# First stage: normalised input at the head of VectorE's turn, mean square a step later, one silu session a pair; scan: the next pair's first inputs formed ahead

## The reference

```
x = x + attn_a(layernorm(x));  x = x + ffn(layernorm(x))
x = x + attn_b(layernorm(x));  x = x + ffn(layernorm(x))

# attn_a, after the input projection (z, xBC, dt):
xBC = silu(causal_conv4(xBC) + conv_b);  x, B, C = split(xBC)
dt = softplus(dt + dt_bias);  A = -exp(A_log)
Y = ssd(x * dt, A * dt, B, C) + D * x        # 4 heads of 64, state 16, by sums over tiles of 128
y = rmsnorm(Y * silu(z)) * norm_w;  return y @ W_out.T

# attn_b (the scan), 256 channels x 16 states:
dt = softplus(x @ Wdt.T + bdt + dt_bias)
A_bar = (1 + dt*A/2) / (1 - dt*A/2);  B_bar = dt / (1 - dt*A/2)
state_t = A_bar_t * state_{t-1} + B_bar_t * B_t * xi_t;  out_t = sum_s state_t[s] * C_t[s]
y = layernorm(out * silu(z)) * gamma + beta;  return y @ Wout.T
```

## Time and profile before

| | |
|---|---|
| time, three runs | 2639.4, 2646.31, 2657.2 us; median 2646.31 |
| the profiled execution | 2651.16 us, its span 2649.4 us |
| busy, share of the span | PE 83%, VectorE 75%, ScalarE 70%, GpSimd 58% |
| mean granted TensorE clock | 0.928; first stage 0.90, scan 0.84 |
| first stage | 0 to 300 us: a turn takes 31.3 to 33.4 us |
| feed-forward | 300 to 1098 us, and 1856 to 2649 us |
| scan | 1098 to 1856 us: a turn takes about 92 us |

### The profile page before, as it was taken

The page is one execution under the profiler, slowest core; times in us unless marked ns, Lnnn a source line. Parts: engine busy times, 40 slices in busy tenths (PEclk is TensorE's granted clock), DMA queues, the critical chain, the costliest instruction groups (busy, mean ns, idle before and its releaser), DMA issues. The chain is left out here.

```text
span 2649.4 us, 46209 instructions
## 1 busy us (share of the span) xinstructions
PE 2192.8 (83%) x13308; PEld 1124.7 (42%) x13308; DVE 1996.1 (75%) x5421; ACT 1856.4 (70%) x4745; POOL 1543.0 (58%) x1364
## 2 busy tenths in 40 slices
PE   5888789999999999667777767776799899999997
PEld 2555445455555555222222222222355455555553
DVE  4666477777777776388998989898677777787774
ACT  3555277778777777488687777776677777777774
POOL 1233276556665665177787677676565556665652
PEclk8999799999999999788888888889999999999999
DMA  3000000000000000000000000000000000000000
GB/s 129 1 0 1 4 13 13 10 14 12 13 13 14 12 9 14 0 0 1 1 1 1 0 1 0 0 1 0 13 13 13 9 14 12 13 17 17 21 13 17
DMA packets 12209, 30.04 MB, mean 11 GB/s; under 512 B 2240, under 2 KB 2240, under 8 KB 11584
## 3 DMA queue, kind: packets, MB, share of 16 engines
q1 hardware_dynamic: 11968, 27.41, 3.8%
HBM read 8.52 MB, written 2.10 MB: 4 GB/s over the span
## 5 line engine op out<-in xcount | busy, mean ns | idle before, releaser
L517 POOL TENSOR_TENSOR arena<-arena 128x512 f32<-128x512 f32 x256 | 325.0, 1270 | 444.8 <-DVE arena L1530 444.8
L575 POOL TENSOR_TENSOR arena<-arena 128x512 f32<-128x512 f32 x256 | 327.7, 1295 | 127.2 <-ACT arena L1257 118.5
L523 POOL TENSOR_TENSOR arena<-arena,SR 128x512 f32<-128x512 f32 x256 | 285.3, 1114 | 109.5 <-ACT SR L1139 108.6
L1610 DVE TENSOR_TENSOR_SCAN arena<-arena,psum 128x512 f32<-128x512 f32 x256 | 311.0, 1215 | 3.2
L929 PE MATMUL psum<-BS,tabs 96*128 96x512 bf16 x384 | 146.1, 442 | 197.1 <-DVE arena L1610 195.3
L997 PE MATMUL psum<-arena,first 128*128 128x512 f32 x512 | 288.8, 653 | 10.9 <-POOL arena L566 10.6
L1536 DVE TENSOR_REDUCE SM<-arena 128x8 f32<-128x512 f32 x256 | 175.6, 686 | 155.9 <-ACT arena L1129 145.5
L530 POOL TENSOR_TENSOR P<-P,RS 128x512 f32<-128x512 f32 x256 | 270.3, 1056 | 35.5 <-DVE RS L1457 35.1
L1129 ACT ACTIVATE arena<-psum 128x512 f32<-128x512 f32 x256 | 151.4, 591 | 186.6 <-PE psum L853 186.5
L853 PE MATMUL psum<-rest,HA 128*128 128x512 f32 x512 | 267.3, 604 | 0.4 <-DVE HA L1445 0.4
L807 PE MATMUL psum<-HN,rest 128*128 128x512 f32 (+1 forms) x384 | 197.0, 640 | 56.0 <-ACT arena L1122 51.0
(11 more groups left out here) (223 smaller groups left out, 5290.8 us busy)
## 6 DMA issues: line engine op xcount, KB each, us to landing
arena<-arena SPq DMA_DIRECT2D x128, 128.0 KB, 2.3
rest<-in_rest SPq DMA_DIRECT2D x1, 4183.0 KB, 20.9
X<-in_x SPq DMA_DIRECT2D x1, 2048.0 KB, 9.0
out<-X SPq DMA_DIRECT2D x8, 256.0 KB, 2.3
tabs<-in_tabs SPq DMA_DIRECT2D x1, 1216.0 KB, 11.5
first<-in_first SPq DMA_DIRECT2D x1, 875.5 KB, 4.5
```

The source lines that it names most:

```text
L517: nc.gpsimd.tensor_tensor(CQ[:, n % 2, :], CQ[:, n % 2, :], SQN[:, n % 2, :], ALU.add).then_inc(f_rope, 1)
L523: nc.gpsimd.tensor_tensor(heads, heads, SR[:, n % 2, :].unsqueeze(2).to_broadcast([128, HEADS, DH]), ALU.mult).then_inc(f_qk, 1)
L575: nc.gpsimd.tensor_tensor(WU[:, k % DEEP, :], RG[:, k % DEEP, :], U[t.j % 2][:, k % 2, :], ALU.mult).then_inc(m_wu, 1)
L1610: v.tensor_tensor_scan(HS[:, k % DEEP, :], AB[:, k % DEEP, :], B_BANK[k % 2], 0.0, ALU.mult, ALU.add).then_inc(m_hs, 1)
```

## The change

In the first stage:
- VectorE forms x times dt and XN at the head of the turn, ahead of the first mask and the first MM product; before, they stood behind MM and the D term.
- PE's mean square (L687) moves from steps 3 and 4 to steps 4 and 5, so that its second half stands behind the second x projection.
- ACT's silu of x moves from step 7 to step 12, into the session of B, C and z; the table loads at step 7 go.

In the scan:
- POOL forms WU of steps 0 and 1 of the next pair at the end of a turn, each ahead of one of the last two odd products.
- PE spreads the next pair's B for steps 0 and 1 and C for state 0 at the end of a turn, ahead of the last three sums.
- VectorE's CEN, HN and the block of L1651 and L1653 move one step later (2 to 3, 8 to 9, 11 to 12).

```diff
@@ POOL, scan
+            def weighted_input(t, k, pair=0):
+                t.wait_ge(m_rg, STEPS, k + 1, pair=pair)
+                t.wait_ge(m_vb, STEPS, k + 1 - DEEP, pair=pair)
+                if k == 0:
+                    t.wait_ge(m_u, 1, 1, pair=pair)
+                nc.gpsimd.tensor_tensor(WU[:, k % DEEP, :], RG[:, k % DEEP, :], U[(t.j + pair) % 2][:, k % 2, :],
+                                        ALU.mult).then_inc(m_wu, 1)
+
             def pool_turn(t):
                 for k in range(STEPS):
                     if t.states:
-                        t.wait_ge(m_rg, STEPS, k + 1)
-                        t.wait_ge(m_vb, STEPS, k + 1 - DEEP)
-                        if k == 0:
-                            t.wait_ge(m_u, 1, 1)
-                        nc.gpsimd.tensor_tensor(WU[:, k % DEEP, :], RG[:, k % DEEP, :], U[t.j % 2][:, k % 2, :],
-                                                ALU.mult).then_inc(m_wu, 1)
+                        if k >= 2:
+                            weighted_input(t, k)
...
-                if t.states:
-                    odd_times_c(t, NS - 2)
-                    odd_times_c(t, NS - 1)
+                for late in range(2):
+                    if t.after:
+                        weighted_input(t, late, pair=1)
+                    if t.states:
+                        odd_times_c(t, NS - 2 + late)
@@ PE, first stage
             def a_pe_ending(t, h):
-                if h in (3, 4):
-                    half = h - 3
+                if h in (4, 5):
+                    half = h - 4
@@ PE, scan
             def pe_turn(t):
                 if t.states:
-                    spread_b(t, 0)
-                    spread_c(t, 0)
-                    spread_b(t, 1)
                     spread_c(t, 1)
...
-                    if t.states and k >= 2:
+                    if t.states and 2 <= k < STEPS - 1:
                         accumulate(t, k - 2)
+                if t.after:
+                    spread_b(t, 0, pair=1)
+                    spread_c(t, 0, pair=1)
+                    spread_b(t, 1, pair=1)
                 if t.states:
-                    accumulate(t, STEPS - 2)
-                    accumulate(t, STEPS - 1)
+                    for k in range(STEPS - 3, STEPS):
+                        accumulate(t, k)
@@ ACT, first stage
-                elif h == 7:
+                elif h == 12:
                     for k in range(2):
                         t.wait_ge(a_cx, 8, 4 * k + 4, pair=1)
                         A(XA[side][:, k, :], XA[side][:, k, :], ACT.Silu, bias=F("a_convb", k, k + 1)).then_inc(a_act, 1)
-                    nc.scalar.preload_act_table_set(EXP_LN)
-                elif h == 12:
@@ VectorE, first stage
                 for h in range(16):
+                    if t.states and h == 0:
+                        x_times_dt(t)
+                    if t.after and h == 0:
+                        a_dve_beginning(t, h)
                     if t.states and h % 2 == 0:
...
-                    if t.states and h == 0:
-                        x_times_dt(t)
                     if t.before:
                         a_dve_ending(t, h)
-                    if t.after:
+                    if t.after and h:
                         a_dve_beginning(t, h)
@@ VectorE, scan
-                if k == 2:
+                if k == 3:
                     t.wait_ge(ln_mean, 1, LN_M + 1, pair=1)
...
-                elif k == 8:
+                elif k == 9:
                     t.wait_ge(ln_rs, 1, LN_M + 1, pair=1)
...
-                elif k == 11:
+                elif k == 12:
                     t.wait_ge(m_exp, 1, 1, pair=1)
```

More of the change, by code:

```diff
@@ L926, in _, with spread, spread_b, spread_c @@
             pe.wait_ge(f_x, PAIRS)
-            def spread(t, s, column, dst, done):
-                mm(dst, T16("sel", 128 * column, 128 * column + 128, p=96), BS[t.j % 2][:, :],
+            def spread(t, column, dst, done, pair):
+                mm(dst, T16("sel", 128 * column, 128 * column + 128, p=96), BS[(t.j + pair) % 2][:, :],
                    start=True, stop=True).then_inc(done, 1)
-            def spread_b(t, k):
-                t.wait_ge(m_hs, STEPS, k - 1)
+            def spread_b(t, k, pair=0):
+                t.wait_ge(m_hs, STEPS, k - 1, pair=pair)
                 if k == 0:
-                    t.wait_ge(m_bs, 3, 3)
-                spread(t, k, k // 2, B_BANK[k % 2], m_bb)
-            def spread_c(t, s):
-                t.wait_ge(m_pce, NS, s - 1)
-                spread(t, s, NS + s, C_BANK[s % 2], m_bc)
+                    t.wait_ge(m_bs, 3, 3, pair=pair)
+                spread(t, k // 2, B_BANK[k % 2], m_bb, pair)
+            def spread_c(t, s, pair=0):
+                t.wait_ge(m_pce, NS, s - 1, pair=pair)
+                spread(t, NS + s, C_BANK[s % 2], m_bc, pair)
             def half_sum(k, weight, source, done):
```

## The result

The changed kernel took 2620.69 us in the median of four runs, against 2650.53 for the kernel before beside it: a ratio of 0.988 (95% interval 0.985 to 0.990), 29.8 us less. I had forecast 33. In a later group of runs the same kernel came to 0.990 (0.987 to 0.994). The profiled execution took 2621.68 us, 29.5 less than the one of before.

The account below looks back on a forecast made before the run. VectorE was taken as nearly full in the scan, no engine full in the first stage. First stage 16 us less, scan 17.2 less (21.2 less 4.0), together 33: from 2646.3 to 2613 us, range 2595 to 2630.

Parts of the forecast that it names:

- first stage: First-stage turns: 16 us less in all, bounds 6 and 22; net 2.1 us in each of six turns.
- scan's border: Borders between scan turns: VectorE's 2.83 us wait goes at five, 7.0 us more at two jumps back; together 21.2 us less.
- shifted beginning: CEN, HN and L1651 a step later in the scan: waits are one 4.0 us slack that only moves; costs 4.0 us.
- L1669's holds: Scan's maximum stays long in five of seven turns; rival that it falls the other way, 2595 or 2620 us, chance 0.10.
- XN at the head: First stage: x times dt and XN fit into VectorE's early waits, so all behind comes 2.1 us sooner a turn.
- the stall: First stage: PE's 1.65 us wait ahead of L656 goes, and full clock is expected where it was 0.59.
- Mean square later: First stage: moving L687's second half behind x projection L662 removes VectorE's wait there, 1.0 us a turn.
- One session: First stage: silus of x in the later session cost 1.4 us a turn on the path; 0.4 us LM wait goes.
- the jumps' 1.3: Scan's two jumps back: VectorE's own instruction fetch comes to light, 1.3 us exposed at each.
- The four places that I listed: Scan turn's middle: where VectorE would wait instead: 1.5 us at WU(11), 1.6 at L1651, 1.7 at WU(17), 1.1 at WU(19).
- The rival in which the waits vanish: Scan turn's middle: the shift does remove VectorE's waits, some 24 us more gained, 2589 us; chance 0.06.
- The slower rival: Scan: POOL holds HN and both halves of L1632 at the port, 3.68 us each; twelve holds give 2657 us; chance 0.03.

Follow-up runs that it names:

- the border alone: Kernel before with only the scan's border edits (POOL's WU and PE's spreads at the turn's end); ratio 0.992, 22.6 us less.
- the shift alone: Kernel before with only CEN, HN and the block of L1651 and L1653 a step later; ratio 1.004, 11 us more.
- the two-operand form: Changed kernel with the maximum L1676 (L1669 before) written as scalar_tensor_tensor over the same operand twice, same values; ratio 0.990.
- the mean square back: Changed kernel with PE's mean square back at steps 3 and 4 of the first stage; ratio 0.992.
- the combined kernel: Changed kernel with TensorE's L671 and L673 ahead of L700, silu of x back at step 7, and no shift; ratio 0.977, 2591.96 us.
- the silu back: Changed kernel with silu of x back at step 7 in its own session, two more table loads a turn; ratio 0.987, 35.5 us less than before.

## Why the prediction was right, and where it was off

| step | forecast | found |
|---|---|---|
| first stage | -16 | -14.6 in the profile |
| scan's border | -21.2 | -24 |
| shifted beginning | +4.0 | +3.3 |
| L1669's holds | 0 | +3.3 (one more) |
| feed-forward stages | 0 | +2.8 and +0.6 |

The rows found add up to -28.6 against -29.5 in the profiles; the missing 0.9 is that the scan before lay 0.9 above the level of its like (736.9 against 736). The stage's -14.6 is one pair of profiles. The six profiles with all three parts end it at 279.5 to 286.9 us, 283.2 in the mean, 16.7 before the 299.9 of the old one. So the sum of 16 was met, but its parts were not right one by one.

*XN at the head* was put at 2.1 us and gave 2.7: the stall went as forecast, and with it the reduced clock behind it, which even the 31.3 us turns had (0.95), and the wait of 1.03 for L662. *Mean square later*: 1.0 forecast, 0.6 found, and the mechanism was wrong: it was to win that wait, which the head had already won; what it did win is two MM products that no longer run beside GpSimd's spreads, in four of six turns. *One session*: -1.4 + 0.4 forecast, a cost of 1.2 found: right, and the only part of the first stage that costs. The net of 2.1 a turn (31.34 to 29.29 is 2.05) was right to the tenth by luck, two errors that cancel. What failed was "if the stall goes I expect full clock there": the stall moved from L656 to L700 and grew to 2.39 us there in turns 1 and 3; these were long by 2.2 us and turn 6 by 1.2. Nor is it chance which: in the six profiles with all three parts turn 3 was long in all and turn 1 in five. In the profiled pair turns 1 to 6 gave 12.1 us of a forecast 13.6, turn 0 gave 3.3 of 1, and from turn 7 on 0.8 were lost where 1.5 should have been won.

*The border*: 2.83 us and the jumps' 1.3 came as forecast (1.36 and 1.38 found). The term was short by some 3 us: I counted none of the 3.5 us that VectorE waited for PE before CEN, as part of a slack that only moves. In the border alone that wait fell to one of 0.39 while the 0.92 to 1.1 for HN stayed as they were. Before, TensorE's clock was 0.50 from 1496 to 1502 us, behind the border's idle stretch and while VectorE waited for CEN's mean; in the border alone it was 1.00 at the same place (1474 to 1488). So the wait belonged to the border and was won with it.

*The shift*: the count of one ACT and POOL chain held. The 4.0 us of waits in a turn's middle became 4.07 at new places. (The four places that I listed, 1.5, 1.6, 1.7 and 1.1, add up to 5.9, which does not agree with one slack of 4.0; found were 0.61, 0.43, 1.75 and 1.08.) With a wait of 0.68 for ScalarE's copy near step 4, in place of CEN's, a turn waited 4.74 instead of the 4.20 of a like turn of the border alone: +0.5 for the +0.4 forecast. Turn 0 was 1.35 us longer than without the shift, at equal holds, for the 1.5 forecast. The rival in which the waits vanish is refuted by the shift alone, which was slower.

*The port*: taken at five of seven turns and 3.68 us a hold; it was six of seven at 3.27, which the share of 0.10 for the rival covered. The slower rival, holds at HN and the inverse root's product, did not come: HN took 0.68 and the two halves of L1639 0.68 and 1.41, as before in all but their order. But its argument that L1669 alone was held, for its form, is wrong: the two-operand form and the next instruction on SBUF were held at the same place.

## What to carry to other kernels

A wait that an edit removes is won only if no other wait of the same engine is fed by the same chain of other engines; add the waits of one turn between two points where that chain starts and ends, and count their sum once. Look on the engine that ends a wait for what stands ahead of the awaited instruction in its queue: an instruction of TensorE that waits at the head of its queue cost more here (1.8 us a turn) than any of the three edits but one gained. And where a stage's time is compared between single profiles, first take out what falls differently from one to the next: here holds of 3.3 us and dropped clocks of 1.2 to 2.2 us a turn, which together were as large as the terms sought. But look first whether they fall in the same turn in every profile, as turn 3's dropped clock did: then it has a cause that an edit can reach, here the stall of 2.39 us.

## What the runs showed of the hardware

At the maximum's place a VectorE instruction with all operands in SBUF, started beside a row of GpSimd instructions without a gap, either got in after the first (1.61 us instead of 0.74) or was done only when the row had ended (5.26). It read one operand (5.26) or two (5.80), on 128 partitions or on 32 (4.60). Its start did not explain which of the two it was. The Trainium skill ("SBUF — State Buffer", Who interferes with whom) says that instructions with two inputs in SBUF contend with a GpSimd instruction that reads SBUF too; the 5.80 and 4.60 agree, and so do the MM products of 0.74 to 0.95 us instead of 0.55 in the first stage. It also says that the one that comes second is blocked for the instruction of the first; that fits the short case, and the held ones, through four GpSimd instructions, contradict it.

TensorE's granted clock fell behind a turn's long idle time, but not each time: after 2.39 us ahead of L700 it fell in turns 1 and 3 of the change (0.95 over the turn) and not in turn 3 of the mean square back (1.00, 29.88 us), nor in turns 4 to 6 of the combined kernel, where as much lay ahead of L676 (1.00). Twice it fell behind 1.79: turn 4 with the silu back (0.94, 29.71 us) and turn 2 with the two-operand form (0.94, 30.95).
